# A two-layer sparse graph attention kernel: layer two's variances taken by VectorE's statistics, x added beside the exponential, the last roots on GpSimd, and a new order of work

## The chip, the core and the metric

The kernel runs on one core of a Trainium2 chip. The metric is the device time of one execution in microseconds (us), the median of several runs. The engines are called as in the profile: PE is TensorE, DVE is VectorE, ACT is ScalarE, POOL is GpSimd, and SP starts plain transfers.

## What is computed

Two graph attention layers over one adjacency matrix of 2048 rows, each followed by a residual and a layer norm over 256 channels. Cut to what matters:

```python
def _layernorm(x, axis=-1, eps=1e-05):
    m = jnp.mean(x, axis=axis, keepdims=True)
    v = jnp.var(x, axis=axis, keepdims=True)
    return (x - m) / jnp.sqrt(v + eps)

# layer one: masked dot-product attention with 8 heads over the edges of adj
scores = jnp.where(adj > 0, einsum('hnd,hmd->hnm', q * SCALE, k), NEG_FILL)
out = einsum('hnm,hmd->hnd', softmax(scores), vv)
x = _layernorm(x + out)
# layer two: h = x W^T + b; scores leaky_relu(s_src[i] + s_dst[j]); softmax over the edges
x = _layernorm(x + elu(einsum('ijh,jhd->ihd', attn, h)))
```

## The kernel before

**Tiles.** The 2048 rows are 16 tiles of 128. About one in 200 entries of the matrix is an edge, so the kernel first turns the matrix into lists of edges (MAX8 on DVE, L1693), and then works on chunks of 128 edges: 73 chunks in 7 groups per layer, a group holding the edges of one to four tiles. A stage is named by its kind, layer, group and piece: prod(0,3,0) is the first piece of the products of group 3 in layer one (layers count from 0).

**Layer one, by chunk and tile.** POOL fetches the rows of k and v that a chunk's edges point at by an indirect transfer, a gather (L1214), into a ring of 24 slots. PE copies the query rows to the edges (L1560), DVE multiplies (prod, L1828), POOL halves the products by an addition (half, L1227) and DVE sums them (score, L1839). PE turns the scores, DVE scans for row ends (L1893 to L1898), ACT takes exponentials, DVE weighs the fetched v (weigh, L1931), and PE adds them up per tile (L1612). Weighing frees the ring slot. For each tile DVE divides and adds x (norm, L1656, L1658, L1650), ACT takes the sum of squares (L1403, L1405), POOL takes the root (shift, L1246 to L1253), ACT normalizes (L1418), PE turns the tile (turn_norm, L1623), ACT copies it, PE multiplies it by W (project, L1634, L1636), ACT copies the result out (evac, L1433) and SP stores it in a table in memory. For the last two tiles DVE normalizes (L1944). The queries of a group need a split of x into a high and a low part, which POOL makes (left_1 and left_2, L1235, L1240). A stage `bad` on POOL (L1290 to L1299) gathers the check whether the lists were long enough.

**Layer two.** POOL gathers from the table (L1214 again, ring of 44 slots), so its first gather waits for the last store of layer one. DVE scores, scans and weighs, PE sums. For each tile: norm_a on DVE (L1656, L1658) divides, ACT takes Relu and Exp (elu, L1438, L1441), norm_b on DVE (L1954 makes the elu, L1650 adds x and sums the row), ACT takes the variance (spread_of_b: L1411 the mean, L1413 the squares). For a pair of tiles ACT guesses the inverse root (L1447, L1449), DVE refines it (refine, four small instructions, L1963 to L1969), and ACT writes the normalized tile (emit, L1457), which SP stores.

**What sets the order.** Each engine runs its stages in one fixed order, made by a list scheduler in the program (`Order`, `all_stages`). It ranks a stage by planned durations and by a table `LATER` that shifts the rank of each kind of stage; `AHEAD` and `FORESIGHT` are two more numbers of it. An engine's block takes the stages in that order, and waits on semaphores for what a stage needs; nothing behind a waiting instruction of the same engine can pass it.

## Time and profile before

| | |
|---|---|
| median of three runs | 341.42 us (338.7 to 343.41) |
| the profiled execution: time, span | 341.08 us, 339.5 us |
| outside the span | 1.58 us |
| busy: DVE, PE, POOL, ACT | 264.3, 223.4, 220.6, 172.6 us |
| mean granted clock of PE | 0.852 |

Durations below come from the profiled execution. Layer one runs to about 222 us, where the first gather of layer two starts; that layer's 73 gathers run to 314.5 us, and the last write ends at 339.5 us. In a row of the timeline the first number is the start, the second the duration (of all instructions of the row, where xN is over 1), and the bracket tells how long the engine had been idle and what ended that; "issue" means that the profile shows no releaser.

### The profile page before, as it was taken

How to read it: one execution, taken by the hardware profiler on the slowest of the kernel's cores; microseconds unless marked ns; L12 is line 12 of the kernel's file. 1: busy time of each engine (PE TensorE's matmuls, PEld its weight loads, DVE VectorE, ACT ScalarE, POOL GpSimd, SP SyncE). 2: the span in 40 equal slices, each digit the busy share in tenths (PEclk: the TensorE clock that was granted, in tenths of full speed). 3: DMA queues.
4: the chain of work that ended last, by engine and by line, in shares of the span. 5: the costliest groups of instructions: out<-in, count | busy, mean ns of one | idle time of the engine just before them, and what ended most of it. 6: DMA issues, size and time to landing. Idle time of an engine off the chain costs nothing.

```text
span 339.5 us, 5180 instructions
## 1 busy us (share of the span) xinstructions
PE 223.4 (66%) x1282; PEld 158.0 (47%) x1282; DVE 264.3 (78%) x760; ACT 172.6 (51%) x473; POOL 220.6 (65%) x354
## 2 busy tenths in 40 slices
PE   0099756648685388688888988761714957758850
PEld 0077433436463156466666755450503734536630
DVE  2998999999999489899999766896416388885981
ACT  4646668352867556668643646200020056764495
POOL 8627867726858776787889771167777777777000
PEclk9999695857799679999999999655585899969995
DMA  7977769945886947453535420024434454554212
GB/s 279 384 193 292 258 209 315 336 163 162 270 298 189 323 160 269 124 156 89 165 93 151 105 70 20 33 84 115 108 108 114 108 141 117 133 146 139 64 36 68
DMA packets 23710, 55.90 MB, mean 165 GB/s; under 512 B 6267, under 2 KB 14587, under 8 KB 21627
## 3 DMA queue, kind: packets, MB, share of 16 engines
q0 software_dynamic: 9392, 29.74, 30.5%
q1 hardware_dynamic: 14283, 25.77, 21.8%
q8 instruction: 13, 0.21, 0.3%
q14 instruction: 22, 0.18, 0.2%
HBM read 51.17 MB, written 4.33 MB: 163 GB/s over the span
## 4 chain that ended last, share of the span: by engine, by line
POOL 13%; PE 12%; issue 12%; DVE 10%; ACT 6%; DMA 2%; DVEq 0%; ACTq 0%; POOLq 0%
POOL e_ring L1214 10%; PE e_po L1612 8%; DMA e_ring<-table,e_col_i 2%; DVE e_left L1931 2%; DVE e_weighted L1931 1%; PE e_pj L1636 1%; POOL e_slot_e L1227 1%; DVE e_y L1658 1%; ACT e_search L1320 1%; DVE e_kept L1693 1%; ACT e_prod L1457 1%; DVE e_run L1893 1%; DVE e_run L1895 1%; DVE e_y L1954 1%; PE e_pt L1623 1%
## 5 line engine op out<-in xcount | busy, mean ns | idle before, releaser
L1214 POOL DMA_INDIRECT e_ring<-in_kv,e_col_i x73 | 71.2, 976 | 32.3 <-issue 16.7
L1214 POOL DMA_INDIRECT e_ring<-table,e_col_i x73 | 70.1, 961 | 23.8 <-issue 22.3
L1612 PE MATMUL e_po<-e_weighted,e_sel_edges 128*128 128x264 f32 x178 | 47.3, 402 | 7.0 <-DVE e_weighted L1931 7.0
L1320 ACT ACTIVATE e_search<-e_search 128x2048 bf16<-128x2048 int32 x16 | 39.9, 2491 | 11.4 <-DMA e_search<-in_adj 7.1
L1612 PEld LDWEIGHTS e_po<-e_weighted,e_sel_edges 128*128 128x128 f32 x178 | 32.7, 195 | 14.0 <-DVE e_weighted L1931 9.0
L1560 PE MATMUL e_pq<-e_left,e_sel_rows 128*128 128x256 bf16 x164 | 35.2, 311 | 0.0
L1693 DVE MAX8 e_kept<-e_search 128x8 f32<-128x1024 f32 x24 | 29.4, 1224 | 0.6
L1612 PE MATMUL e_po<-e_left,e_search 128*128 128x264 f32 x92 | 27.3, 452 | 1.7 <-DVE e_left L1931 1.7
L1931 DVE TENSOR_TENSOR e_weighted<-e_ring,e_pc 128x528 f32<-128x528 f32 (+1 forms) x40 | 26.0, 669 | 2.6 <-PE e_pc L1592 1.9
L1599 PE MATMUL e_po<-e_mean_row,e_diagonal 128*128 128x264 f32 x64 | 22.4, 436 | 8.3 <-DVE e_y L1658 7.9
L1356 ACT ACTIVATE e_diagonal<-e_ident,e_filled 128x128 f32<-128x128 f32 x32 | 12.5, 398 | 28.5 <-DVE e_y L1658 28.1
L1560 PE MATMUL e_pq<-e_xres,e_sel_rows 128*128 128x256 bf16 x82 | 25.8, 314 | 0.4 <-DVE e_prod L1853 0.4
L1612 PEld LDWEIGHTS e_po<-e_left,e_search 128*128 128x128 f32 x92 | 20.5, 228 | 6.8 <-DVE e_left L1931 2.6
L1379 ACT COPY e_sel_edges<-e_pt 128x512 f32<-128x512 f32 (+1 forms) x23 | 12.3, 537 | 21.9 <-PE e_po L1612 13.6
L1828 DVE TENSOR_TENSOR e_prod<-e_pq,e_ring 128x512 f32<-128x512 f32 (+1 forms) x27 | 16.3, 634 | 8.1 <-issue 4.9
L1560 PEld LDWEIGHTS e_pq<-e_left,e_sel_rows 128*128 128x128 bf16 x164 | 17.9, 109 | 5.8 <-issue 0.6
L1227 POOL TENSOR_TENSOR e_slot_e<-e_prod 128x256 f32<-128x256 f32 (+1 forms) x27 | 18.5, 702 | 1.6 <-DVE e_prod L1828 1.4
L1395 ACT ACTIVATE e_weight_t<-e_shifted 88x128 f32<-88x128 f32 (+5 forms) x14 | 4.3, 306 | 29.8 <-DVE e_shifted L1898 21.7
L1235 POOL TENSOR_TENSOR e_left<-e_xres 128x256 f32<-128x256 f32 (+3 forms) x7 | 8.1, 1163 | 13.8 <-PE e_pq L1560 7.5
L1599 PEld LDWEIGHTS e_po<-e_mean_row,e_diagonal 128*128 128x128 f32 x64 | 10.5, 196 | 13.3 <-issue 12.4
L1650 DVE SCALAR_TENSOR_TENSOR e_y<-e_y,e_xres 128x256 f32<-128x256 f32 x32 | 14.8, 462 | 1.1
L1585 PE MATMUL e_pc<-e_ident,e_score 128*88 128x128 f32 (+5 forms) x30 | 5.8, 309 | 14.7 <-DVE e_score L1880 10.0
(240 smaller groups left out, 586.3 us busy)
## 6 DMA issues: line engine op xcount, KB each, us to landing
e_search<-in_adj SPq DMA_DIRECT2D x16, 1024.0 KB, 7.1
table<-e_hx SPq DMA_DIRECT2D x16, 136.0 KB, 1.8
e_ring<-in_kv SPq DMA_DIRECT2D x1, 2112.0 KB, 13.3
out<-e_prod SPq DMA_DIRECT2D x16, 128.0 KB, 2.3
e_ring<-in_kv,e_col_i POOLq DMA_INDIRECT x73, 4.1
e_ring<-table,e_col_i POOLq DMA_INDIRECT x73, 2.8
e_xres<-in_x SPq DMA_DIRECT2D x2, 384.0 KB, 9.8
e_xres<-in_x SPq DMA_DIRECT2D x1, 512.0 KB, 8.0
```

Of the source, the lines that this page charges most:

```text
L1214: nc.gpsimd.indirect_dma_start(out=rings[layer][:, q % RING[layer], :], out_offset=None, in_=kv if layer == 0 else table, in_offset=bass.I ...
L1227: nc.gpsimd.tensor_tensor(halves[:, pair % 2, at:at + m * C // 2].rearrange("p (h d) -> p h d", d=D // 2), products[:, :, 0:D // 2], produ ...
L1320: nc.scalar.activation(val_signs[:, k % 2, :], adj_tile[:, k % 2, :], ACT.Sign, accum_out=signs[:, k:k + 1]).then_inc(s("sgn_ready"), 1)
L1356: nc.scalar.activation(diagonal[:, n % 3, :], ident[:], ACT.Copy, scale=filled[:, at:at + 1]).then_inc(s("diagonal_ready"), 1)
L1379: nc.scalar.copy(selection(0, u, m).rearrange("p c r -> p (c r)"), pt[:, 0:m * P]).then_inc(s("turns_copied"), 1)
L1560: last = nc.tensor.matmul(pq[b % 2][:, j * C:(j + 1) * C], sel(u), upper(x_parts[part])[:, 0, :], start=(u == some[0][0] and part == 0), s ...
L1599: nc.tensor.matmul(po[n % 2][:, 0:CV], diagonal[:, n % 3, :], mean_row[:], start=True, stop=False)
L1612: last = nc.tensor.matmul(po[n % 2][:, 0:CV], selection(layer, u, 1)[:, 0, :], weighted[plan.weighed_into(b)][:, j * CV:(j + 1) * CV], sta ...
L1650: return v.scalar_tensor_tensor(out=y[:, k % 4, :], in0=y[:, k % 4, :], scalar=1.0, in1=xres[:, plan.tile_of(layer, k), :], op0=ALU.mult, ...
L1693: last = v.max(to, segs[:, i])
L1828: v.tensor_tensor(prod[:, i % 2, 0:m * C].rearrange("p (c k) -> p c k", c=m), pq[b % 2][:, 0:m * C].rearrange("p (c k) -> p c k", c=m), ri ...
L1931: v.tensor_tensor(weighted[plan.weighed_into(b)][:, 0:m * CV].rearrange("p (c h d) -> p c h d", c=m, d=D1), rings[layer][:, at:at + m, lo: ...
```

## The change

**Layer two.** The stage spread_of_b on ACT is gone. A new DVE stage plus_x adds max(y, 0) to x as soon as norm_a is done, while ACT works on the exponential; norm_b then adds the exponential less one, and takes mean and variance by two statistics instructions, BN_STATS and BN_AGGR (`take_moments`). norm_a of tile k now waits for elu of tile k-4 and no longer for its emit. For the last four tiles a POOL stage `roots` takes the place of guess and refine, and the emit of the last tile is done by DVE.

**Layer one.** The last two tiles take their moments by the same two instructions on DVE, not on ACT. The turn of the last tile is put ahead of the projection of the one before it.

**Order.** `AHEAD`, `FORESIGHT` and the whole table `LATER` have new values (two entries are shown).

```diff
-AHEAD = 11.4
+AHEAD = 11.255
-FORESIGHT = 1.4357
+FORESIGHT = 1.2927
-LATER = {("back", 0): -0.93, ("back", 1): 1.71, ...
+LATER = {("back", 0): -4.69, ("back", 1): 0.94, ...
...
-            put("PE", 1.35 if k < 13 else 2.2, rank - 0.2, ("project", k), ("copy_norm", k), None if bank is None else ("evac", k - 1) ...
+            put("PE", 1.35 if k < 13 else 2.2, rank - 0.2, ("project", k), ("copy_norm", k), ("turn_norm", NK - 1) if k == NK - 2 else None, ...
...
-            put("DVE", 0.7, rank - 0.2, ("norm_a", k), end, ("emit", k - 4) if k >= 4 else ("normed", NK - 4 + k))
+            put("DVE", 0.7, rank - 0.2, ("norm_a", k), end, ("elu", k - 4) if k >= 4 else ("normed", NK - 4 + k))
+            put("DVE", 0.44, rank - 0.2, ("plus_x", k), ("norm_a", k))
...
+def alone(k):
+
+    return k >= len(SLOTS) - 4
...
+                elif stage[0] == "roots":
+                    k = stage[1]
+                    one = slice(k % 4, k % 4 + 1)
+                    pool.wait_ge(s("z_ready"), NT + k + 1)
+                    pool.wait_ge(s("emitted"), k - 3)
+                    own.did(nc.gpsimd.tensor_scalar(var_eps[:, one], moments[:, k % 4, 1:2], EPS, None, ALU.add))
+                    own.wait()
+                    if k == NT - 1:
+                        nc.gpsimd.tensor_tensor(rstd[:, one], var_eps[:, one], minus_half[:], ALU.pow).then_inc(s("rooted"), 1)
+                        continue
...
-                elif stage[0] == "spread_of_b":
-                    k = stage[1]
-                    one = slice(k % 4, k % 4 + 1)
-                    act.wait_ge(s("z_ready"), NT + k + 1)
-                    own.did(nc.scalar.activation(neg_mean[:, one], total[:, one], ACT.Copy, scale=-1.0 / C))
-                    own.wait()
-                    nc.scalar.activation(elu[:, k % 2, :], y[:, k % 4, :], ACT.Square, bias=neg_mean[:, one], accum_out=squares[:, one]).then_inc(s("var_ready"), 1)
...
+            def take_moments(k, z):
+                st.did(v.bn_stats(stats[:, k % 4, :], z))
+                st.wait()
+                v.bn_aggr(moments[:, k % 4, :], stats[:, k % 4, :]).then_inc(s("z_ready"), 1)
...
+                elif stage[0] == "plus_x":
+                    k = stage[1]
+                    z = xres[:, plan.tile_of(1, k), :]
+                    st.did(v.scalar_tensor_tensor(out=z, in0=y[:, k % 4, :], scalar=0.0, in1=z, op0=ALU.max, op1=ALU.add))
                 elif stage[0] == "norm_b":
                     k = stage[1]
                     dve.wait_ge(s("elu_ready"), k + 1)
-                    v.scalar_tensor_tensor(out=y[:, k % 4, :], in0=elu[:, k % 2, :], scalar=-1.0, in1=y[:, k % 4, :], op0=ALU.add, op1=ALU.max).then_inc(s("elu_used"), 1)
+                    if k >= 4:
+                        dve.wait_ge(s("guess_ready"), k // 2 - 1)
+                    st.wait()
+                    z = xres[:, plan.tile_of(1, k), :]
+                    v.scalar_tensor_tensor(out=z, in0=elu[:, k % 2, :], scalar=-1.0, in1=z, op0=ALU.add, op1=ALU.add).then_inc(s("elu_used"), 1)
                     dve.wait_ge(s("elu_used"), k + 1)
-                    with_x(1, k).then_inc(s("z_ready"), 1)
+                    take_moments(k, z)
+                elif stage[0] == "emit" and stage[1] == NT - 1:
...
+                    dve.wait_ge(s("rooted"), 4)
+                    dve.wait_ge(out_stored[k % 2], 16 * (k // 2))
+                    v.tensor_scalar(y_out[:, k % 2, :], xres[:, plan.tile_of(1, k), :], moments[:, k % 4, 0:1], rstd[:, one], ALU.subtract, ALU.mult).then_inc(s("last_emitted"), 1)
```

**First place: POOL in the middle of layer one.** The rows are POOL's instructions in program order; L1227 and L1241 are the halves, L1214 and L1228 the gathers, L1235/L1240 and L1249/L1254 the split of x for a later group, and the three one-column rows are the root of a tile. Before, from the last halves of group 2's second piece to those of its last piece:

```order
L1227 TENSOR_TENSOR e_slot_e<-e_prod 128x256 x2
L1235 TENSOR_TENSOR e_left<-e_xres 128x768
L1240 TENSOR_TENSOR e_left<-e_left 128x768
L1214 DMA e_ring<-in_kv,e_col_i 128x520 x3
L1246 TENSOR_SCALAR e_var_eps<-e_norms 128x1
L1251 TENSOR_TENSOR e_rstd<-e_var_eps,e_minus_half 128x1
L1253 TENSOR_TENSOR e_shift<-e_norms,e_rstd 128x1
L1214 DMA e_ring<-in_kv,e_col_i 128x520
L1227 TENSOR_TENSOR e_slot_e<-e_prod 128x256
L1227 TENSOR_TENSOR e_slot_e<-e_prod 128x128
```

With the change:

```order
L1241 TENSOR_TENSOR e_slot_e<-e_prod 128x256 x2
L1228 DMA e_ring<-in_kv,e_col_i 128x520 x6
L1241 TENSOR_TENSOR e_slot_e<-e_prod 128x256
L1241 TENSOR_TENSOR e_slot_e<-e_prod 128x128
L1264 TENSOR_SCALAR e_var_eps<-e_norms 128x1
L1269 TENSOR_TENSOR e_rstd<-e_var_eps,e_minus_half 128x1
L1271 TENSOR_TENSOR e_shift<-e_norms,e_rstd 128x1
L1228 DMA e_ring<-in_kv,e_col_i 128x520 x4
```

The three gathers and the one behind them (35 to 38, group 3's first four) and two more now stand right behind the halves; the two split instructions have moved behind the next tile's root, and the root behind the halves.

**Second place: POOL at the end of layer one.** The same engine around the last group's halves; L1290 to L1299 (L1321 to L1330) are the stage `bad`. Before:

```order
L1296 TENSOR_TENSOR e_end<-e_end,e_caps 128x16
L1297 TENSOR_SCALAR e_bad<-e_found_n 128x16
L1299 TENSOR_SCALAR e_bad<-e_end 128x16
L1227 TENSOR_TENSOR e_slot_e<-e_prod 128x256 x2
L1227 TENSOR_TENSOR e_slot_e<-e_prod 128x128
```

With the change:

```order
L1241 TENSOR_TENSOR e_slot_e<-e_prod 128x256 x2
L1336 TENSOR_TENSOR e_src_parts<-e_src_parts 128x24
L1338 TENSOR_TENSOR e_src_parts<-e_src_parts 128x24
L1264 TENSOR_SCALAR e_var_eps<-e_norms 128x1
L1269 TENSOR_TENSOR e_rstd<-e_var_eps,e_minus_half 128x1
L1271 TENSOR_TENSOR e_shift<-e_norms,e_rstd 128x1
L1241 TENSOR_TENSOR e_slot_e<-e_prod 128x128
L1321 TENSOR_TENSOR e_end<-e_mid,e_half 128x16
```

The eight instructions of `bad` stood ahead of the last group's halves and now stand behind them.

**Third place: PE between the layers.** The turns of the last two tiles (L1623, L1650, e_xres) and their projections (L1634/L1636, L1661/L1663); L1571 and L1598 spread source terms to the edges. Before:

```order
L1623 MATMUL e_pt<-e_ident,e_xres 128x128 x2
L1634 MATMUL e_pj<-e_w_sb 128x280
L1636 MATMUL e_pj<-e_w_ext,e_xt 128x280 x2
L1623 MATMUL e_pq<-e_ident,e_xres 128x128 x2
L1571 MATMUL e_pt<-e_src_parts,e_sel_rows 128x24 x16
L1634 MATMUL e_pq<-e_w_sb 128x280
L1636 MATMUL e_pq<-e_w_ext,e_count 128x280 x2
```

With the change:

```order
L1650 MATMUL e_pt<-e_ident,e_xres 128x128 x2
L1650 MATMUL e_pq<-e_ident,e_xres 128x128 x2
L1661 MATMUL e_pj<-e_w_sb 128x280
L1663 MATMUL e_pj<-e_w_ext,e_xt 128x280 x2
L1661 MATMUL e_pq<-e_w_sb 128x280
L1663 MATMUL e_pq<-e_w_ext,e_count 128x280 x2
L1598 MATMUL e_pt<-e_src_parts,e_sel_rows 128x24 x16
```

The last turn stands ahead of the projection of tile 14, and the spread of 16 small products no longer stands between the two projections.

## Rows read from the trace of the kernel before

**Rows 1.** Busy time by stretch: stretch, its length, PE, PEld, DVE, ACT, POOL, clock
```profile
0.00:170.00 170.00, 112.98 (x756) 80.20 (x757) 147.83 (x399) 103.40 (x239) 119.68 (x217) 0.88 0.70 232
...
300.00:325.00 25.00, 19.89 (x73) 13.98 (x73) 20.44 (x57) 12.51 (x39) 11.19 (x12) 0.86 0.34 94
```
**Rows 2.** The gathers' line L1214: layer two's shortest/median/longest, and the landing
```profile
L1214 POOL DMA_INDIRECT e_ring<-table,e_col_i x73: 942/946/1250, 222.5 to 313.6; - x73
...
DMA to landing us min/median/max: 2.7/3.5/9.0
```
**Rows 3.** Timeline, POOL: layer two's first and last gather
```profile
222.46 1.20 POOL L1214 DMA_INDIRECT e_ring<-table,e_col_i  x1 [1.90 <-issue]
...
313.60 0.94 POOL L1214 DMA_INDIRECT e_ring<-table,e_col_i  x1 [0.30 <-issue]
```
**Rows 4.** Timeline, DVE, the two halves of prod(0,3,0) in the middle of layer one
```profile
112.43 0.69 DVE L1828 TENSOR_TENSOR e_prod<-e_pq,e_ring 128x512 f32<-128x512 f32 x1
117.99 0.69 DVE L1828 TENSOR_TENSOR e_prod<-e_pq,e_ring 128x512 f32<-128x512 f32 x1 [4.88 <-issue]
```
**Rows 5.** Timeline, POOL ahead of that: halves, left_1, gather 35, gather 38
```profile
95.19 1.45 POOL L1227 TENSOR_TENSOR e_slot_e<-e_prod 128x256 f32<-128x256 f32 x2
100.44 1.47 POOL L1235 TENSOR_TENSOR e_left<-e_xres 128x768 f32<-128x768 f32 x1 [3.80 <-DMA e_xres<-in_x]
...
103.66 0.97 POOL L1214 DMA_INDIRECT e_ring<-in_kv,e_col_i  x1 [0.15 <-issue]
...
108.88 1.07 POOL L1214 DMA_INDIRECT e_ring<-in_kv,e_col_i  x1 [0.56 <-DVE e_weighted L1931]
```
**Rows 6.** The page's DMA issues: layer one's gathers, median us to landing
```profile
e_ring<-in_kv,e_col_i POOLq DMA_INDIRECT x73, 4.1
```
**Rows 7.** Timeline, end of layer one: POOL's last halves, DVE behind them
```profile
198.84 1.89 POOL L1227 TENSOR_TENSOR e_slot_e<-e_prod 128x256 f32<-128x256 f32 x3
...
199.70 0.42 DVE L1828 TENSOR_TENSOR e_prod<-e_pq,e_ring 128x256 f32<-128x256 f32 x1 [1.31 <-POOL e_slot_e L1227]
```
**Rows 8.** Timeline between the layers: normed 15, project 14, turn 15, project 15, evac 15
```profile
213.09 0.41 DVE L1944 TENSOR_SCALAR e_xres<-e_y,e_norms,e_rstd 128x256 f32<-128x256 f32 x1 [0.77 <-POOL e_rstd L1249]
...
213.84 1.33 PE L1636 MATMUL e_pj<-e_w_ext,e_xt 128*128 128x280 f32 x4
214.96 0.63 PE L1623 MATMUL e_pq<-e_ident,e_xres 128*128 128x128 f32 x2
...
216.88 0.41 PE L1634 MATMUL e_pq<-e_w_sb 3*128 3x280 bf16 x1
...
219.53 0.39 ACT L1433 COPY e_hx<-e_pq 128x272 f32<-128x272 f32 x1 [3.27 <-issue]
```
**Rows 9.** Groups by line and shape: busy us, mean ns of one
```profile
L1812 DVE SCALAR_TENSOR_TENSOR e_hit<-e_slot_e,e_rel 128x256 f32<-128x256 f32 x16 | 10.1, 630 | 1.6 <-issue 0.4
...
L1839 DVE TENSOR_REDUCE e_score<-e_slot_e 128x16 f32<-128x256 f32 x1 | 0.4, 414 | 0.0
...
L1721 DVE TENSOR_REDUCE e_full<-e_raw 128x1 f32<-128x8 f32 x2 | 0.3, 167 | 0.1
...
L1710 DVE TENSOR_SCALAR e_hit<-e_val 128x256 f32<-128x256 f32 x1 | 0.3, 295 | 0.0
...
L1246 POOL TENSOR_SCALAR e_var_eps<-e_norms 128x1 f32<-128x1 f32 x16 | 3.2, 201 | 8.8 <-ACT e_count L1405 4.5 <-ACT e_xt L1405 3.3
...
L1249 POOL TENSOR_TENSOR e_rstd<-e_var_eps,e_minus_half 128x1 f32<-128x1 f32 x2 | 1.1, 550 | 0.2
```
**Rows 10.** Timeline, the end: norm_b 15, refine 7, emit 15
```profile
331.45 0.43 DVE L1650 SCALAR_TENSOR_TENSOR e_y<-e_y,e_xres 128x256 f32<-128x256 f32 x1
...
334.26 0.16 DVE L1963 SCALAR_TENSOR_TENSOR e_guessed<-e_norms,e_guess 128x2 f32<-128x2 f32 x1 [2.38 <-ACT e_guess L1449]
...
335.87 0.60 ACT L1457 ACTIVATE e_prod<-e_y,e_shift,e_rstd 128x256 f32<-128x256 f32 x1 [0.23 <-issue]
```
**Rows 11.** Timeline, DVE, one of layer one's small waits for POOL
```profile
142.55 1.02 DVE L1828 TENSOR_TENSOR e_prod<-e_pq,e_ring 128x512 f32<-128x512 f32 x2 [0.86 <-POOL e_slot_e L1227]
```

More of the change, by code:

```diff
@@ new lines @@
+LATER = {("back", 0): -4.69, ("back", 1): 0.94, ("copy_mean", 0): 0.08, ("copy_mean", 1): 7.98, ("diagonal", 0): 19.08,
+         ("diagonal", 1): 0.03, ("exp", 0): 5.74, ("exp", 1): -0.11, ("fill", 0): 4.26, ("fill", 1): -0.92, ("gather", 0): 2.18,
+         ("gather", 1): 2.1, ("scan", 0): 0.02, ("scan", 1): 14.06, ("score", 0): -1.57, ("score", 1): -0.45, ("sums", 0): 2.35,
+         ("sums", 1): 14.26, ("turn", 0): -3.72, ("turn", 1): -2.01, ("weigh", 0): 6.78, ("weigh", 1): -0.27, "add_src": 1.65,
+         "bad": 0.02, "bad_sum": -5.35, "check": 13.99, "choose": -2.09, "column_sums": 4.03, "copy_big": -5.38, "copy_edges": 3.29,
+         "copy_norm": 3.11, "copy_pens": 5.43, "count": -5.36, "elu": -18.39, "emit": -25.38, "evac": 20.21, "far": -1.36,
+         "filled": -2.01, "find": -8.36, "find_big": -10.39, "flags": 4.95, "guess": -0.76, "half": -2.59, "left_1": -0.25,
+         "left_2": -0.99, "load": -7.31, "mean_h": 5.3, "mean_v": 72.47, "move": 9.22, "move_big": 4.8, "norm": -1.34, "norm_a": 4.61,
+         "norm_b": 0.53, "normed": 21.18, "out": -0.71, "pack": -9.28, "place": 0.32, "plus_x": 24.4, "prefix": 0.49, "prod": -1.67,
+         "project": 3.43, "queries": -4.05, "refine": -13.89, "roots": -2.3, "rows": 26.71, "select": 5.78, "shift": -22.35,
+         "sign": -0.71, "split_b": -1.6, "spread": 7.38, "spread_of": 2.59, "store": 1.87, "sum_w": -1.64, "turn_edges": -11.83,
+         "turn_norm": -12.27, "turn_pens": 1.88, "turn_src": 12.43, "v": -28.34, "w": 45.38, "x": 12.17}
@@ L980, in edge_pass @@
         xts = [sb("e_xt", [P, C]), count0]
+        stats = sb("e_stats", [P, 4, 6])
+        moments = sb("e_moments", [P, 4, 2])
         norms = sb("e_norms", [P, 3, 4])
@@ L1968, in _ @@
                     st.wait()
-                    v.tensor_tensor(shift[:, two], neg_mean[:, two], rstd[:, two], ALU.mult).then_inc(s("refined"), 1)
+                    v.scalar_tensor_tensor(out=shift[:, two], in0=moments[:, two, 0], scalar=-1.0, in1=rstd[:, two], op0=ALU.mult, op1=ALU.mult).then_inc(s("refined"), 1)
                     dve.wait_ge(s("refined"), j + 1)
```

91 lines of the change are left out of this document (51 added, 40 removed).

## Prediction

> **What bounds the kernel now.** I read the busy times by stretch first, to see which engine is full where; then the line of the gathers, for layer two; then DVE's and POOL's timelines at DVE's longest waits.
>
> In layer one DVE is the bound: 147.8 of the first 170 us, against 119.7 on POOL and 113.0 on PE [rows 1]. There a wait of DVE costs its length, and a shuffle of other engines' work costs nothing unless it makes DVE wait.
>
> Layer two is bound by its gathers until they end. All 73 take 0.94 to 1.25 us [rows 2], the first starts at 222.46 and the last at 313.60 [rows 3]: 91.1 us over 72 steps is 1.27 each, one behind the other, and the wait ahead of one is "issue", not a ring slot. So layer two starts when the last store of layer one has landed, its gathers take 92 us whatever DVE does, and an engine's work is free there if it is done by the last chunk. Then comes a tail of 25 us in which DVE is full again, 20.4 of 25 us from 300 [rows 1].
>
> So three places set the end: DVE's waits in layer one, the bridge from the last tile to the first gather, and the tail. I sum against the profiled execution's own 341.08 us (span 339.5 and 1.58 outside it); it lies 0.3 under the median of 341.42, so the sum is the forecast of the median within that.
>
> **The change, part by part.**
>
> *A. The middle of layer one.* DVE's longest wait there is 4.88 us ahead of the second half of prod(0,3,0) [rows 4], which multiplies chunk 38. Gather 38 is issued at 108.88 [rows 5]; the longest landing of a gather is 9.0 us [rows 2], and 108.88 + 9.0 = 117.9 is where the product starts. It was late because POOL, done with its halves at 95.19 + 1.45 = 96.64, stood 3.80 us waiting for x's next part before left_1, and then did left_1 and left_2 before gather 35 at 103.66 [rows 5]. With the change gathers 35 to 40 stand right behind the halves, the split behind shift 1. From 96.64 at 1.25 each, 38 could go at 100.4; I take 103, since the ring's slots come free only as DVE weighs. By the reordered queue DVE reaches the product at about 109.7. At the median landing of 4.1 [rows 6] the rows are there at 107.1 and the wait is gone: −4.9. At 9.0 again they land at 112.0 and 2.3 us remain: −2.6. I take −4.9: six gathers that no longer come in a crowd behind a stopped queue are nearer to the median than to the longest landing. The split that moved back is covered: group 4's products start at 142.55 [rows 11], 26 us after its new place (about 116.5: six gathers, halves, a root, four gathers, two halves, flags, a root and 3.0 us of split behind 96.64).
>
> *B. The end of layer one.* DVE waits 1.31 us for the last group's halves [rows 7], which stand on POOL behind `bad`. The halves now go first; `bad` has no reader before the end of the layer's bridge. −1.3; bounds 0 (the halves wait for the products anyway) and −1.3.
>
> *C. The bridge.* Turn 15 starts at 214.96 behind projection 14, projection 15 at 216.88 behind the spread products, evac 15 at 219.53, the first gather 2.93 us after that [rows 8, 3]. But normed 15, which turn 15 needs, ends at 213.09 + 0.41 = 213.50, and projection 14 at 215.17 [rows 8]. With the turn ahead of projection 14, turn 15 runs at 213.5, its copies are done while projection 14 runs, and projection 15 follows at 215.2 rather than 216.88: −1.7. Moments on DVE put 0.41 + 0.16 on each of the two tiles (prices below), but save ACT's squares, so normed 15 stays where it was within 0.1. I take −1.4, as the copies share ACT with evac 14; bounds 0 (copy late) and −1.7.
>
> *D. Layer two's tiles and the tail.* Neither BN_STATS nor BN_AGGR is in the trace. BN_STATS reads 256 elements a partition: below, a one-source operation on 256, 0.295; above, the accumulating one on 256, 0.63; I take the reduction of 256, 0.41, as the nearest in kind [rows 9]. BN_AGGR reads six numbers: 0.17 as a reduction of eight [rows 9]. plus_x and the sum in norm_b are the 0.43 to 0.46 of norm_b's instruction [rows 10]. Per tile DVE did 0.43 + 0.46 = 0.89 and now does 0.45 + 0.46 + 0.41 + 0.04 + 0.16 = 1.52: +0.63. Ten tiles' worth lies ahead of the score of the last but one group in the new order, beside the gathers; DVE has room there, and I put +0.5 for what it delays. Six come after it: +3.8. Refine runs twice before the last norm_b instead of three times, −0.8 (four of 0.16 with gaps). Two waits for turned scores, covered before, lie open: +0.6 as an estimate of 0.3 each. So norm_b 15 ends 4.1 later than 331.88 [rows 10], at 336.0 in old time.
>
> From there to the end of emit 15 it was 336.47 − 331.88 = 4.6 us: ACT's means and squares of two tiles, guess, refine (DVE waited 2.38) and two emits [rows 10]. Now it is POOL's 0.20 and 0.55 [rows 9] with 0.17 for two handovers, then DVE's emit of 0.41 as L1944 [rows 8] and 0.1: 1.4. So −3.2, and D is +4.1 − 3.2 = **+0.9**. With BN_STATS at 0.295 six tiles give −0.7, D is +0.2; at 0.63 they give +1.3, D is +2.2.
>
> *E. New waits.* The whole order of layer one is new. Waits of DVE of the size of 0.86 and 1.31 [rows 11, 7] are what such an order leaves; I allow **+1.3**, one or two of them, between 0 and +2.6.
>
> *Spread_of_b on ACT*, 0.9 a tile, is removed at no gain besides the tail: ACT is not full in layer two (12.5 of 25 us [rows 1]).
>
> **Sum:** 341.08 − 4.9 − 1.3 − 1.4 + 0.9 + 1.3 = **335.7 us**.
>
> **A lock that would speak against it.** DVE's comparisons (one source each) run beside the first gathers of layer two, its weighing (two sources) beside the last; yet the slowest of the 73 took 1.25 us against a median of 0.946, and the last 0.94 [rows 2, 3]. So no operation of DVE has held a gather up by more than 0.30, nearly all by nothing, and I put the moments' effect on POOL at 0. The Trainium skill (SBUF — State Buffer, "🔬 SBUF: two separate sides") says that a DVE operation in a two-port mode locks GpSimd out of a shared port, so that a gather's descriptors cannot be written. By that rule ten BN_STATS beside the gathers would each hold one up; the trace agrees only to the 0.30 above. Which mode BN_STATS uses no row here shows, so the hold-up is a rival.
>
> **The rivals.**
>
> 1. *No new waits, and some old ones go too.* The small waits behind A are a lottery that the new table draws again. For it: DVE's idle time from 120 to 200 comes in pieces like rows 11. Without E and with two of them gone (2.3): 335.7 − 1.3 − 2.3 = **332.1**.
>
> 2. *The stall moves.* Gather 38 lands in time, but DVE, 4.9 us ahead, meets the next late transfer or half: the gathers behind it keep POOL's pace. For it: POOL is at 70% in the same stretch [rows 1] and ring slots are freed by DVE's own weighing. A is worth nothing: 335.7 + 4.9 = **340.6**; with half of it, 338.2.
>
> 3. *Slower: the moments hold up the gathers.* If each of the ten BN_STATS beside gathers costs POOL one more issue of 0.95 [rows 2], the last gather is 9.5 us later, and 335.7 + 9.5 = **345.2**. It decides from 0.54 us a tile on (5.4 gained, ten tiles). Against it: no operation beside the gathers has cost one more than 0.30.
>
> 4. *The tail only.* BN_STATS far above 0.63 would be paid six times at the end; 5.4 us are used up at 0.9 more, at 1.3 us each. Against it: no row on 256 elements is above 0.63.
>
> **Chances.** My forecast, between 333.5 and 338: 0.50. Rival 1, 330 to 333.5: 0.19. Rival 2, 338 to 342: 0.25. Rivals 3 and 4, above 342: 0.06. To leave out no more than 2 in 10 the range goes from 331.5 to 341.0: it takes in A at −2.6 (338.0), BN_STATS at either bound (335.0, 337.0) and rival 2. It holds faster and unchanged alike, so the likeliest case's own range stands beside it: 333.5 to 338. 2% of 341.4 is 6.8 us, about what a measurement of this kernel can tell from no change; faster by that is below 334.6: rival 1 and a third of the forecast's case, 0.19 + 0.17 = 0.36. Slower is above 348.2: 0.02. The rest, 0.62, is within 2%.
>
> **What the changed profile would show.** A: gather 38 at about 103, no DVE wait over 1 us ahead of prod(0,3,0); if one stands there, the landing was the cause, and if it stands a group later, rival 2. B: the last halves ahead of `bad`, and no wait for them on DVE. C: turn 15 before projection 14, evac 15 about 1.4 us nearer to normed 15. D: BN_STATS near 0.41 and BN_AGGR near 0.17; norm_b 15 to the last emit 1.4 us; gathers still 1.25 apart and the stretch from the first gather to the last 91 us (rival 3 if more); from the last gather to the end of the last emit 336.47 − 313.60 + 0.9 = 23.8 us. I would be wrong if layer one ends less than 4 us earlier, or if DVE falls behind the gathers so far that they wait for ring slots.

## The result

| | before | changed |
|---|---|---|
| median of four runs | 340.62 us (338.70 to 343.41) | 345.46 us (343.39 to 347.10) |
| ratio, with its 95% interval | | 1.0139 (1.0090 to 1.0187) |
| the profiled execution: time, span | 341.08, 339.5 us | 344.15, 342.4 us |
| busy: DVE, PE, POOL, ACT | 264.3, 223.4, 220.6, 172.6 us | 276.9, 226.1, 226.4, 159.0 us |

I had forecast 335.7 us, and the changed kernel is 1.4% slower. Both halves of the picture changed: layer two does start earlier, by 4.0 us of the 6.3 I had summed, and everything behind its last gather takes 6.8 us longer, where I had written 0.9. These are the rows of the changed kernel that answer to [rows 3] and [rows 10]. First its timeline: POOL's first and last gather, and what DVE does from the score of the last but one group to the last write.

```profile
218.47 1.12 POOL L1228 DMA_INDIRECT e_ring<-table,e_col_i  x1 [1.64 <-issue]
...
309.84 0.94 POOL L1228 DMA_INDIRECT e_ring<-table,e_col_i  x1 [0.30 <-issue]
...
310.45 0.25 DVE L1908 TENSOR_TENSOR e_score<-e_src,e_ring 128x88 f32<-128x88 f32 x1 [0.41 <-issue]
...
334.21 0.18 DVE L1679 BATCH_NORM_AGGREGATE e_moments<-e_stats 128x2 f32<-128x6 f32 x1
...
335.50 0.41 DVE L2008 TENSOR_SCALAR e_prod<-e_xres,e_moments,e_rstd 128x256 f32<-128x256 f32 x1 [1.11 <-POOL e_rstd L1280]
```

In the kernel before, the same score and the end of the last moments (ACT's squares followed) stand here:

```profile
311.24 0.25 DVE L1876 TENSOR_TENSOR e_score<-e_src,e_ring 128x88 f32<-128x88 f32 x1 [0.17 <-issue]
...
331.80 0.08 DVE L1650 DVE_READ_ACCUMULATOR e_y<-e_y,e_xres 128x1 f32 x1
```

Then the instructions that close the changed program, from the view of the line that holds them all (count, shortest/median/longest in ns, start; "q" is an engine's sequencer):

```profile
L2048 POOLq DRAIN  x1: 6362/6362/6362, 335.8 to 335.8; - x1
L2048 ACTq DRAIN  x1: 81/81/81, 337.0 to 337.0; - x1
L2048 DVEq DRAIN  x1: 58/58/58, 338.6 to 338.6; - x1
L2048 SPq DRAIN  x1: 53/53/53, 338.8 to 338.8; - x1
```

The last write ends at 335.91, earlier than the 336.47 of before. SP has stored it and is done at 338.8. But the span ends at 342.44, 0.23 us behind POOL's closing instruction, a DRAIN that takes 6.36 us from 335.85, to 342.21. In the kernel before, whose lines follow, POOL was through with its last gather at 314.55 and closed at 320.92, 6.37 later, in the shade of the tail; there the span ended 0.21 us behind SP's DRAIN.

```profile
L1997 POOLq DRAIN  x1: 8793/8793/8793, 312.1 to 312.1; - x1
...
L1997 SPq DRAIN  x1: 53/53/53, 339.2 to 339.2; - x1
```

With the roots, POOL's last work is among the last of all.

The difference of the two spans, stretch by stretch (us, from the two timelines):

| stretch | before | changed | difference | my sum |
|---|---|---|---|---|
| to the first gather of layer two | 222.46 | 218.47 | −3.99 | −6.3 |
| first gather to last gather | 91.14 | 91.37 | +0.23 | 0 |
| last gather to the score of the last but one group | −2.36 | +0.61 | +2.97 | +0.5 |
| that score to the last moments | 20.64 | 23.94 | +3.30 | +3.6 |
| last moments to the end of the last write | 4.59 | 1.52 | −3.07 | −3.2 |
| last write to the end of the span | 2.98 | 6.53 | +3.55 | 0 |
| **sum** | 339.45 | 342.44 | **+2.99** | −5.4 |

Two rows carry the miss of the tail: the score comes 2.97 later against the gathers, and the end 3.55 later against the last write. The first row is the miss of layer one. And the medians lie 4.84 apart where the profiled executions lie 3.07: of the four changed runs two took 343.4 and 344.2, two 346.8 and 347.1, and the profiled one is of the shorter pair. Ratios here and below leave out executions that took over 1.5% longer than the fastest of the same kernel. The experiments take these one by one.

### The profile page after: what moved, and what is told of

The parts are those of the page before. It is cut to its first block, busy times and chain, and to the rows that moved or that the text cites. A ratio compares the mean times of both kernels' runs of the same rounds, so it can differ in the third digit from the quotient of the medians.

```text
span 342.4 us, 5152 instructions
## 1 busy us (share of the span) xinstructions
PE 226.1 (66%) x1282; PEld 159.9 (47%) x1282; DVE 276.9 (81%) x773; ACT 159.0 (46%) x414; POOL 226.4 (66%) x365
## 4 chain that ended last, share of the span: by engine, by line
DVE 28%; PE 19%; POOL 10%; issue 9%; ACT 1%; DMA 1%; DVEq 1%; POOLq 0%; ACTq 0%
PE e_po L1639 11%; POOL e_ring L1228 7%; DVE e_kept L1725 3%; PE e_pj L1663 3%; DVE e_y L1690 2%; DVE e_weighted L1963 2%; DVE e_prod L1860 2%; DVE e_stats L1677 2%; DVE e_xres L1999 2%; DVE e_run L1925 2%; DVE e_run L1927 1%; DVE e_left L1963 1%; DVE e_rden L1688 1%; DVE e_xres L1991 1%; PE e_po L1626 1%
## 5 line engine op out<-in xcount | busy, mean ns | idle before, releaser
L1228 POOL DMA_INDIRECT e_ring<-in_kv,e_col_i x73 | 71.8, 983 | 32.3 <-issue 18.6
L1228 POOL DMA_INDIRECT e_ring<-table,e_col_i x73 | 70.4, 964 | 23.6 <-issue 21.7
L1639 PE MATMUL e_po<-e_weighted,e_sel_edges 128*128 128x264 f32 x178 | 50.0, 418 | 9.1 <-DVE e_weighted L1963 9.1
L1639 PEld LDWEIGHTS e_po<-e_weighted,e_sel_edges 128*128 128x128 f32 x178 | 34.1, 204 | 16.4 <-DVE e_weighted L1963 11.1
L1639 PE MATMUL e_po<-e_left,e_search 128*128 128x264 f32 x92 | 31.4, 503 | 1.8 <-DVE e_left L1963 1.8
L1639 PEld LDWEIGHTS e_po<-e_left,e_search 128*128 128x128 f32 x92 | 23.2, 258 | 8.2 <-DVE e_left L1963 2.8
L1461 ACT ACTIVATE e_left<-e_y 128x256 f32<-128x256 f32 x16 | 6.6, 411 | 33.1 <-DVE e_y L1690 33.1
L1241 POOL TENSOR_TENSOR e_slot_e<-e_prod 128x256 f32<-128x256 f32 (+1 forms) x27 | 18.5, 705 | 0.7 <-DVE e_prod L1860 0.4
L1510 PE MATMUL e_pl<-e_slot_hi,e_sel_rows 128*128 128x20 bf16 (+2 forms) x82 | 5.2, 175 | 18.0 <-DVE e_slot_lo L1800 9.4
L1249 POOL TENSOR_TENSOR e_left<-e_xres 128x256 f32<-128x256 f32 (+3 forms) x7 | 8.2, 1167 | 12.6 <-PE e_pq L1587 10.3
L1688 DVE RECIPROCAL e_rden<-e_po 128x8 f32<-128x8 f32 x32 | 6.5, 204 | 11.3 <-PE e_po L1639 10.7
```

Of the source, the lines that this page charges most:

```text
L1228: nc.gpsimd.indirect_dma_start(out=rings[layer][:, q % RING[layer], :], out_offset=None, in_=kv if layer == 0 else table, in_offset=bass.I ...
L1241: nc.gpsimd.tensor_tensor(halves[:, pair % 2, at:at + m * C // 2].rearrange("p (h d) -> p h d", d=D // 2), products[:, :, 0:D // 2], produ ...
L1639: last = nc.tensor.matmul(po[n % 2][:, 0:CV], selection(layer, u, 1)[:, 0, :], weighted[plan.weighed_into(b)][:, j * CV:(j + 1) * CV], sta ...
L1688: st.did(v.reciprocal(rden[:], sums[:, :, D]))
```

## The experiments

**1. POOL's closing instruction, taken away and added.** The changed kernel without its roots on POOL, and the kernel before with one POOL instruction late:

```diff
 def alone(k):
-    return k >= len(SLOTS) - 4
+    return False
...
-                    dve.wait_ge(s("rooted"), 4)
+                    dve.wait_ge(s("refined"), NT // 2)
```

> The changed kernel without the roots on POOL: guess and refine to the last tile, everything else as changed (DVE still writes the last tile). Theory: the end is held by POOL, whose closing instruction took 6.36 us behind its last root (335.85 to 342.21, span 342.4). With no root, POOL closes behind the last gather, at about 310.7 + 6.4 = 317, and the end goes by the last write: the last moments at 334.4, ACT's guess 0.8, refine 0.75, the write 0.4 and handovers, so 336.5, and 3.0 behind it as before: a span of 339.6, a time near 341.3, against 344.15 for the changed kernel's own profile. Rival: the stretch behind the last write is long because DVE writes it and loads its flag just ahead of it; then the span is 342.4 + 0.7 = 343.1 and POOL has nothing to do with it.

```diff
+            pool.wait_ge(s("refined"), NT // 2)
+            nc.gpsimd.memset(var_eps[:, 0:1], 0.0)
```

> The kernel before with one more POOL instruction behind its last gather: a memset of one column that waits for the last refine (335.0 in the profile of before); nothing reads it. Theory (POOL's closing instruction costs 6.4 us behind POOL's last work, whatever that was): POOL's last work ends at 335.3, it closes at 341.7, span 341.9 instead of 339.5, time 343.5. Rival (the end goes by the last store alone): span 339.5 and time 341.1, as the memset lies beside the last write.

The closing instructions of POOL in these two, the first without the roots, the second of before with the late memset, and the memset itself:

```profile
L2048 POOLq DRAIN  x1: 7768/7768/7768, 309.6 to 309.6; - x1
```

```profile
L2000 POOLq DRAIN  x1: 6362/6362/6362, 337.9 to 337.9; - x1
```

```profile
336.88 0.10 POOL L1310 MEMSET e_var_eps<- 128x1 f32 x1 [20.68 <-DVE e_shift L1972]
```

Without the roots POOL closes at 317.38, 6.37 behind its last gather, and the end goes by the store again: 3.18 us from the last write to the end of a span of 341.20. The median is 343.05, ratio 1.0057 (1.0011 to 1.0102), against 1.0139. My figure of 339.6 for the span was 1.6 too low: guess and refine put 2.9 us between the last moments and the last write, not 2.1, and a pair's refine stands ahead of them, +0.8. So the roots on POOL shorten the chain by 2.1 us (338.02 − 335.91; 1.9 when counted from the last gather) and lengthen the end by 3.35.

The memset of 0.10 us makes POOL close at 337.86 + 6.36 = 344.22 in a span of 344.45; the last write of that run ended at 338.28, so the end lies 6.17 behind it, where it was 2.98. It moved the end by 3.2 us, though nothing reads what it writes. The one execution took 346.08 us where I had expected 343.5: layer two started 1.36 us later than in the profile of before, and the DRAIN began 0.88 us behind the memset. Both rivals are out: the end does not go by the last store alone, and DVE's write and flag are not what lengthens it. What made POOL late was once its roots and once a memset; other work of POOL was not tried.

**2. Is the late score made by the ten tiles' statistics?** BN_STATS on 8 channels in the first ten tiles (their variances are then those of 8 channels):

```diff
-            def take_moments(k, z):
-                st.did(v.bn_stats(stats[:, k % 4, :], z))
+            def take_moments(k, z, few=False):
+                st.did(v.bn_stats(stats[:, k % 4, :], z[:, 0:8] if few else z))
...
-                    take_moments(k, z)
+                    take_moments(k, z, few=k < 10)
```

> The changed kernel, but in the first ten tiles of layer two BN_STATS reads 8 of the 256 channels, so that their variances are those of 8 channels; the last six tiles are whole. Theory: the ten tiles ahead of the score of the last but one group are not hidden beside the gathers; they make DVE late, so that this score starts 0.65 us behind the start of the last gather, where it stood 2.36 ahead of it in the kernel before. Ten times (0.43 - 0.17) = 2.6 us less work then puts the score 2 to 2.6 us nearer and the end with it: span about 340.0. Rival: the score is late for PE's sums and the new order of weighing, not for the statistics; then it stays where it was against the last gather, within 0.3, and the span stays at 342.4.

```profile
308.94 0.25 DVE L1908 TENSOR_TENSOR e_score<-e_src,e_ring 128x88 f32<-128x88 f32 x1 [0.42 <-issue]
...
310.99 0.95 POOL L1228 DMA_INDIRECT e_ring<-table,e_col_i  x1 [0.30 <-ACT e_prod L1484]
```

Timeline of that run: the score now stands 2.05 ahead of the last gather, where it stood 0.61 behind it. That is 2.66 us for 2.6 us of work taken away (BN_STATS took 0.17 us instead of 0.43 in ten tiles), and the end moved with it: 29.94 us behind the start of the last gather instead of 32.60. As far as these two profiles go, the statistics of the first ten tiles cost the end their full length. The span was 340.93 and not the 340.0 I had written, with a first gather 1.2 us later.

**3. Code or order?** The change has two halves that can be crossed: the code, and the three sets of numbers that set the order. Each alone:

```diff
 # the kernel before, with
-AHEAD = 11.4
+AHEAD = 11.255
-FORESIGHT = 1.4357
+FORESIGHT = 1.2927
-LATER = {("back", 0): -0.93, ...
+LATER = {("back", 0): -4.69, ...
```

> The kernel before with the three sets of numbers of the changed one (AHEAD, FORESIGHT, LATER) and no other edit, so that only the order of work is new. Theory: the 4.0 us by which layer two started earlier (first gather 218.5 instead of 222.5) are the order's for the most part (the wait of 4.88 is gone by it), and the tail of before is kept: first gather at 219 to 220.5, span 336.5 to 338, ratio 0.99. Rival: the gain is the code's at the end of layer one (moments on DVE, turn of the last tile first); then the first gather stays at 221.5 to 222.5 and the ratio at 1.00.

> The changed kernel with the three sets of numbers of the kernel before, so that its code is new and its order goes by the old table. Theory: the late tail comes with the code (plus_x and the statistics on DVE, the root on POOL), not with the order: the score of the last but one group starts 0 to 1 us behind the start of the last gather, the end is 31.5 to 33 us behind the last gather's start, POOL closes 6.36 us behind its last root; and the bridge is short with the code alone, so the first gather is at 218.5 to 220.5. Span 341.5 to 344. Rival: the new order made the tail; then the score stands 2 us ahead of the last gather and the end is 29 to 30 us behind it, span near 339.5.

The four profiles side by side (us; the last three columns count from the start of the last gather, or from what their head says):

| code | numbers | first gather | score | last gather to end | last write to end | ratio |
|---|---|---|---|---|---|---|
| old | old | 222.46 | −2.36 | 25.85 | 2.98 | 1 |
| old | new | 223.67 | −1.84 | 27.76 | 3.00 | 1.0112 (1.0076 to 1.0149) |
| new | old | 221.23 | −2.10 | 30.39 | 6.53 | 1.0144 (1.0081 to 1.0208) |
| new | new | 218.47 | +0.61 | 32.60 | 6.53 | 1.0139 (1.0090 to 1.0187) |

Either half alone is as slow as both. The tail has 4.5 to 4.8 us of the code and 1.9 to 2.2 of the numbers, and they add up within 0.3 us; 3.55 of the code's part is POOL's close. With the old numbers the ten tiles' statistics are hidden as I had said (the score moves by 0.26, and the last write stands 23.86 behind the last gather, +0.99 to before's 22.87; I had +0.9). With both, the score comes 2.97 later, where the code alone moved it by 0.26 and the numbers alone by 0.52: the new numbers use up that room, and then the statistics lie open. Both of my expectations fell. The new numbers were to bring layer two's start forward and to keep the tail of before; alone they bring the start 1.2 us later and the end of the tail 1.9 us later. And the late score was to come with the code; with the old numbers it came 2.10 ahead of the last gather, as the rival had it, and the first gather at 221.23, later than the 218.5 to 220.5 that I had.

**4. Layer two's numbers alone.** The changed kernel with the numbers of layer two's stages as before:

> The changed kernel with the numbers of layer two's stages in LATER as before (plus_x and roots as changed). Theory: the score of the last but one group moves from 0.6 us behind the start of the last gather to about 2 ahead of it, as in the run with the whole old table, and the end from 32.6 to 30.4 us behind that start; POOL still closes 6.36 us behind its last root, so the span is 340 to 341 (first gather 218.5 to 219.5). Rival: the lateness of DVE is of the code, and the score stays within 1 us of the last gather: span 342 to 343.

The score starts at 308.46, 1.98 ahead of the last gather at 310.44, so the same code is not late with layer two's old numbers. The end lies 31.45 behind the last gather's start, not the 30.4 I had; POOL's DRAIN took 6.36 us as in the changed kernel, and the time of the one execution was 343.51. So layer two's numbers are worth 1.15 of the 2.2 us at the end (32.60 − 31.45). The other 1.06, to the 30.39 with all old numbers, goes with those that this run left new, AHEAD, FORESIGHT and layer one's; how is open.

**5. What made layer two start earlier?** The bridge alone, in the kernel before:

```diff
-            ..., ("copy_norm", k), None if bank is None else ("evac", k - 1) ...
+            ..., ("copy_norm", k), ("turn_norm", NK - 1) if k == NK - 2 else None, None if bank is None else ("evac", k - 1) ...
```

> The kernel before with one constraint for the scheduler: the turn of the last tile stands ahead of the projection of tile 14 (the order of a few neighbouring stages in the last 30 us of layer one shifts with it; all else is as before). Theory: of the changed kernel's 4.0 us at the first gather nearly all is this bridge: from the start of normed 15 to evac 15 it took 6.44 us before and 3.67 in the changed kernel, where PE's granted clock stayed at 1.00 instead of 0.65 and projection 15 took 1.21 us instead of 2.23. The tail of before is kept (25.9 us from the start of the last gather to the end). First gather 219 to 220, span 336 to 337.3, ratio 0.991. Rival: the 4.0 us are from DVE's moments in the last two tiles and from the wait removed in the middle; then the first gather stays at 221.5 to 222.5 and the ratio at 1.00.

Ratio 1.0010 (0.9977 to 1.0043), first gather 222.20: nothing gained, though PE does what the change has it do. Compare the two bridges, first that run's and then that of the changed kernel: normed 15, the two projections, evac 15.

```profile
212.51 0.41 DVE L1945 TENSOR_SCALAR e_xres<-e_y,e_norms,e_rstd 128x256 f32<-128x256 f32 x1 [0.57 <-POOL e_rstd L1250]
...
214.82 2.23 PE L1637 MATMUL e_pj<-e_w_ext,e_xt 128*128 128x280 f32 x4
...
217.33 1.90 PE L1637 MATMUL e_pq<-e_w_ext,e_count 128*128 128x280 f32 x4
...
219.26 0.39 ACT L1434 COPY e_hx<-e_pq 128x272 f32<-128x272 f32 x1 [1.68 <-PE e_pq L1637]
```

```profile
211.88 0.41 DVE L1981 TENSOR_SCALAR e_xres<-e_y,e_moments,e_rstd 128x256 f32<-128x256 f32 x1 [0.58 <-POOL e_rstd L1267]
...
212.94 1.21 PE L1663 MATMUL e_pj<-e_w_ext,e_xt 128*128 128x280 f32 x4
...
214.30 1.21 PE L1663 MATMUL e_pq<-e_w_ext,e_count 128*128 128x280 f32 x4
...
215.55 0.39 ACT L1456 COPY e_hx<-e_pq 128x272 f32<-128x272 f32 x1 [0.86 <-PE e_pq L1663]
```

A projection takes 1.21 us in one and 2.23 and 1.90 in the other. The busy times by stretch, of the changed kernel, of the bridge alone, and of the new code with the old numbers, end in three numbers: PE's granted clock, the share of time in which the DMA engines were busy, and GB/s:

```profile
212.00:216.00 4.00, 3.55 (x28) 2.29 (x28) 4.00 (x22) 1.99 (x12) 0.33 (x1) 1.00 0.15 51
```

```profile
212.00:216.00 4.00, 3.15 (x22) 1.98 (x23) 2.68 (x13) 1.25 (x8) 0.92 (x3) 0.50 0.11 35
```

```profile
212.00:216.00 4.00, 3.51 (x10) 1.59 (x8) 3.55 (x18) 1.42 (x9) 0.58 (x3) 0.60 0.00 0
```

In the changed kernel PE keeps its full clock (2.4 GHz) until 221.2, behind the bridge; in the bridge alone it has half of it (1.2 GHz) from 211.9, in the kernel before from 214.8. Over all profiles of this study the time from normed 15 to evac 15 falls into two groups: 3.66 or 3.67 us in the seven where the clock fell at 219.8 or later, and 6.1 to 7.5 us in those where it fell between 211.9 and 214.8, whichever kernel it was. The two kernels of experiment 7 below make the cleanest pair, as both have the changed kernel's layer one, instruction for instruction: 3.67 us in the profile of the first, with the full clock until 221.5, and 6.21 in that of the second, with half of it from 213.96. These are turn 14 (the last turn but one of the bridge), the two projections and evac 15 of the second:

```profile
213.18 0.44 PE L1649 MATMUL e_pt<-e_ident,e_xres 128*128 128x128 f32 x2 [0.89 <-DVE e_xres L1980]
...
215.13 2.23 PE L1662 MATMUL e_pj<-e_w_ext,e_xt 128*128 128x280 f32 x4
...
217.63 2.23 PE L1662 MATMUL e_pq<-e_w_ext,e_count 128*128 128x280 f32 x4
...
219.91 0.39 ACT L1459 COPY e_hx<-e_pq 128x272 f32<-128x272 f32 x1 [2.01 <-PE e_pq L1662]
```

So the clock alone was worth 2.54 us of that bridge. Why it falls ahead of the bridge or behind it is open. PE stood still ahead of turn 14 for 1.56 us in the bridge alone and for 1.41 in the kernel before, and for 0.89 in the changed kernel. But it stood still for the same 0.89 in both profiles of the pair, and in the old code with the new numbers (experiment 3) the clock fell at 213.62 with no wait there. All that can be said is a count: of the eight profiles with the changed kernel's layer one, two of them with idle transposes added, seven kept the full clock through the bridge, and of the six with another layer one none did.

**6. Parts of the change that cost DVE nothing.** The bridge and the last write by DVE beside ACT's write of tile 14, no statistics:

```diff
-            put("ACT", 0.52, rank - 0.3, ("emit", k), ...
+            put("DVE" if k == NK - 1 else "ACT", 0.42 if k == NK - 1 else 0.52, rank - 0.3, ("emit", k), ...
```

> The kernel before with two parts of the change that cost DVE next to nothing: the last turn ahead of projection 14, and the write of the last tile by DVE beside ACT's write of tile 14 (ACT loads its flag ahead of that). No statistics, no plus_x, nothing on POOL in the tail. Theory: the bridge gives 2.5 to 3 as in the run beside it, and the end 0.8 more (the last write ended at 336.47, 1.43 behind refine; with both engines it is over 0.6 behind it): span 335.3 to 336.5, ratio 0.985 to 0.990. Rival: the last store, not the last write, sets the end, since two stores issued together share the queue: then it ends as the run beside it, within 0.3.

Ratio 0.9989 (0.9962 to 1.0017). The tail is 26.5 us from the last gather, not shorter. The last write ended at 338.01 and its store was issued at 339.83, 1.82 later, where SP was 0.80 behind ACT's write before: between the two stores SP loads its flag. The gain of 1 to 1.5% that I had expected did not come, and the rival holds for the end: SP sets it.

**7. New layer one, old tail.** With layer one instruction for instruction as changed, layer two's tiles as before; first with the old numbers for layer two's stages, then with the new ones:

```diff
 # the changed kernel, in layer two
-            put("DVE", 0.44, rank - 0.2, ("plus_x", k), ("norm_a", k))
-            put("DVE", 1.0, rank - 0.2, ("norm_b", k), ("elu", k), ("plus_x", k), ...
+            put("DVE", 0.84, rank - 0.2, ("norm_b", k), ("elu", k))
+            put("ACT", 0.87, rank - 0.3, ("spread_of_b", k), ("norm_b", k))
...
```

> The changed kernel's layer one, instruction for instruction, with layer two's tiles as in the kernel before (variances by ACT, guess and refine to the end, no plus_x, no root on POOL, ACT writes the last tile), and the numbers of layer two's stages in LATER as before. Theory: the changed kernel's early start of layer two (first gather at 218.5 to 219.7 in three profiles) and the tail of before (25.9 to 26 us from the start of the last gather to the end) add up: span 335.5 to 337, ratio 0.985 to 0.992. Rival: the early start needs DVE's statistics only in layer one and is kept, but the tail of before was short only because its gathers came later (DVE is the bound of the whole of layer two, so that an earlier first gather does not bring the end forward); then the score of the last but one group starts behind the last gather, and the span is 338.5 to 339.5, ratio 1.00.

> As the run beside it, but the numbers of layer two's stages in LATER as changed too, so that only the code of layer two's tiles is as before. Theory: the new numbers cost the tail about 2 us with the old code too (27.8 us from the start of the last gather to the end where only the numbers were new, 25.9 where neither was): span 337 to 339, 1.5 to 2 more than the run beside it. Rival: the tail's 2 us there came from something else in that kernel (a late bridge), and both runs have the same tail within 0.5.

Profile of the first: first gather 218.64, score 2.35 ahead of the last gather, end 27.07 behind it, span 337.56, the shortest of the study (I had expected 335.5 to 337). Its times, though, fall into two groups, eight of 338.5 to 340.2 and four of 342.5 to 343.9, and the ratio is 0.9972 (0.9936 to 1.0008): no difference that can be told from none. The second gave 0.9991 (0.9951 to 1.0031); the two intervals overlap, so that what the numbers cost the tail is not settled by this pair. The profile of the second is that of its longest execution, 344.21 us, and is the one with the bridge of 6.21 us above.

**8. Keeping PE busy.** Seven transposes that nothing reads, where PE would wait for normed 14 and 15, in that kernel and in the changed one:

```diff
                     k = stage[1]
+                    if k >= NT - 2:
+                        pe.wait_ge(s("queries_read"), plan.batch0[1, 0])
+                        for j in range(5 if k == NT - 2 else 2):
+                            nc.tensor.transpose(norm_bank(NT - 1)[:, 0:P], ident[:], ident[:])
                     pe.wait_ge(s("normed"), k + 1)
```

> The run with the new layer one and the old tail, with seven transposes of the identity more on PE that nothing reads (five ahead of the wait for normed 14, two ahead of the wait for normed 15), 0.2 us each at full clock, so that PE does not stand idle there. Theory: that kernel's times fall into two groups (338.5 to 340.2 and 342.5 to 343.9) because PE's granted clock falls to half either ahead of the bridge or behind it; with PE kept busy it stays full through the bridge: the upper group goes, all times within 338 to 341, ratio 0.990 to 0.995, first gather 218.5 to 219.7. Rival: the groups have another cause (transfers that land late in layer one); then a third of the times stays above 342.

> The changed kernel with the same seven transposes. Its four times were 343.4 and 344.2, and 346.8 and 347.1. Theory: the upper two are executions in which PE's clock fell ahead of the bridge; with PE kept busy nearly all times are 343 to 344.7, ratio near 1.007, so that of the slowdown of 1.39% about half is the clock's and the rest the tail's. Rival: a third or more of the times stays above 346.

In the first no time of the upper group came: twelve times of 339.7 to 341.9, three of them above the 341 that I had set. It is paid for at the lower end, where the shortest time is 339.69 instead of 338.53, and the ratio stays 0.9972 (0.9940 to 1.0004), not the 0.990 to 0.995 I had. In the changed kernel the rival's condition came true: four of six times are 343.9 to 344.9 and two, a third, are 346.5 and 346.7, ratio 1.0101 (1.0048 to 1.0153). That the clock in the bridge makes the spread of these kernels fits the profiles and the first run; it is not shown, since four long times in twelve against none in twelve may be chance, and the second run leaves a part of the spread open.

## Why the prediction was wrong, step by step

**What bounds the kernel** was read rightly for two of three stretches: layer two's gathers run one behind the other at 1.27 us (91.37 us from first to last, 91.14 before), and an earlier first gather brings the last one forward by as much. Rival 3, the hold-up of gathers by the statistics, did not come: the slowest of the 73 took 1.24 us and the median 0.947. Of the rule that I cited there (the Trainium skill, "SBUF — State Buffer", "🔬 SBUF: two separate sides") no effect of BN_STATS on a gather is seen here.

**A, the wait of 4.88 us,** went as I had said: gather 38 is issued at 103.39, and the two halves of the product run at once. This is the row that answers to [rows 4]:

```profile
110.05 1.29 DVE L1860 TENSOR_TENSOR e_prod<-e_pq,e_ring 128x512 f32<-128x512 f32 x2
```

But normed 15, at the end of layer one, came only 1.21 earlier (213.09 to 211.88), for A, B and E together, which I had summed to 4.9. **The step that failed** is the sentence that in layer one a shuffle of other engines' work costs nothing unless it makes DVE wait. These are DVE's busy times up to normed 15, of the kernel before and of the changed one (stretch, its length, DVE, then clock and DMA as above):

```profile
0.00:213.09 213.09, 180.54 (x481) 0.90 0.62 202
```

```profile
0.00:211.88 211.88, 184.85 (x484) 0.90 0.62 203
```

DVE's idle time fell from 32.55 to 27.03, by 5.5 us, which is more than my 4.9. Its busy time grew by 4.3, which I had put at nothing. The statistics of the last two tiles are 1.2 of it. The other 3.1 are the same instructions, as many as before, taking longer. Between 60 and 211 us the kernel before has six instructions of DVE that took over 0.2 us longer than the shortest of their kind in any profile, and they lost 2.8 us; the changed kernel has 13, and they lost 6.0. All six, and 12 of the 13, ran beside arithmetic on POOL (the last section shows one). No run took that arithmetic away, so that it is the cause of the whole 3.1 is read from the rows and not shown.

The idle time includes a new wait of 2.45 us near the end of layer one, for weights that PE had not turned because ACT took the exponential late, behind a normed that waited for POOL's root:

```profile
186.33 0.60 ACT L1441 ACTIVATE e_xres<-e_y,e_shift,e_rstd 128x256 f32<-128x256 f32 x1 [1.74 <-POOL e_shift L1271]
...
188.80 0.31 ACT L1426 ACTIVATE e_weight_t<-e_shifted 88x128 f32<-88x128 f32 x1
...
190.03 1.32 DVE L1963 TENSOR_TENSOR e_weighted<-e_ring,e_pc 128x528 f32<-128x528 f32 x2 [2.45 <-PE e_pc L1619]
```

Rival 2, the stall that moves, came true in that one wait, but it is not what took the gain. Four profiles of the old code, in which DVE, ACT and POOL have the same order up to 200 us (before, experiments 1, 6 and 5), say the same of the old wait: it was 4.88, 1.80, 2.55 and under 0.5 us, and normed 15 started at 213.09, 213.44, 214.27 and 212.51. The end of layer one does not follow that wait.

**B** showed no wait for the last halves any more, but its 1.31 is inside the same 1.21.

**C, the bridge,** had the right sign, half of the size that was measured (−1.4 for −2.77), and the wrong reason. My sum moved projection 15 forward and left it as long as it was, 2.23 us at half clock. With the clock fallen, the new order took 6.75 us in the bridge alone and 6.21 in the second kernel of experiment 7, against 6.44 before. So 2.54 of the 2.77 are the clock of the profiled execution (6.21 to 3.67). My sum did not have the clock, and that the term came out larger than forecast was luck.

**D, the tail,** failed in two steps: "+0.5 for ten tiles beside the gathers", and the close of POOL, which I had put at nothing. Its prices were near. BN_STATS took 0.428 and BN_AGGR 0.182 (I had 0.41 and 0.16), plus_x 0.417:

```profile
L1677 DVE BATCH_NORM_STATS2 e_stats<-e_xres 128x6 f32<-128x256 f32 x16 | 6.8, 428 | 0.6
...
L1991 DVE SCALAR_TENSOR_TENSOR e_xres<-e_y,e_xres 128x256 f32<-128x256 f32 x16 | 6.7, 417 | 0.3
L1679 DVE BATCH_NORM_AGGREGATE e_moments<-e_stats 128x2 f32<-128x6 f32 x18 | 3.3, 182 | 0.6
```

The six open tiles cost +3.30 (I had +3.6) and the shorter chain gave −3.07 (−3.2). "+0.5 for ten tiles beside the gathers" holds with the old numbers (+0.26) and became +2.97 with the new ones: I priced the new code in the old order's room. And the work moved to POOL was costed as a chain of 0.9 us alone, where its close added 3.55 to the end. I read POOL's idle tail as free, and did not look at what each engine does between its last instruction and the end of the span; the 6.37 us of its closing stood in the trace of before, hidden behind the tail, in a line that is not counted as busy.

**E, +1.3 for new waits,** was large enough: 6.2 us of waits were to go, 5.5 of idle time went, so that new waits took 0.7 net, though one of 2.45 came in one piece.

With the terms as measured (1.21 for A, B and E together) the sum is 341.08 − 1.21 − 2.77 + 0.23 + 2.97 + 3.30 − 3.07 + 3.55 = 344.08, and 344.15 was the profiled time (the rest lies outside the spans). The median, 345.46, is 1.3 us above that execution; its other executions were not profiled.

## What to carry to other kernels

Before work is moved to an idle engine late in a program, look at how that engine closes: here POOL's close ended 6.7 us behind the end of its last root and 7.2 behind that of a late memset, so that POOL's last work must be over that long before the end. A wait of the busiest engine is worth its length only if the engine's busy time stays as it was: compare busy and idle time up to the same instruction, and look through other profiles of the same code in which the wait happens to be shorter. And code and order are to be priced together: room beside a bound is there only in the order in which it was read.

## What was not expected of the hardware

POOL's DRAIN took 6.362 us in each of the six profiles with late POOL work, and began 0.38 us behind the last root or 0.88 behind the memset. It ended 6.37 us behind the last gather in the eight without. The closing DRAINs of ACT, DVE and SP took 0.05 to 0.09.

PE's granted clock decides the bridge by 2.5 us with the same instructions (3.67 us at full clock, 6.21 at half of it). It fell ahead of the bridge in seven of 14 profiles and behind it in the other seven, and with the same layer one and the same waits of PE ahead of the last two turns it did either.

Small instructions of DVE can be held while POOL adds. In the changed kernel a CAST of 60 numbers a partition, which takes 0.19 to 0.34 us in other places and profiles, took 1.04 and ended 0.06 behind an addition on POOL that had started first:

```profile
120.23 1.52 POOL L1254 TENSOR_TENSOR e_left<-e_left 128x768 f32<-128x768 f32 x1
...
120.77 1.04 DVE L1798 CAST e_slot_hi<-e_slots 128x60 bf16<-128x60 f32 x1
```

The eight profiles in which that addition started 0.54 us ahead of this CAST all have it at 1.03 to 1.04 us; in the changed kernel with the old tail and the idle transposes (experiment 8), with no arithmetic of POOL beside it, it took 0.19. The Trainium skill ("SBUF — State Buffer", "🔬 SBUF: two separate sides") says that the port pair shared by DVE and GpSimd is held for a whole instruction by whichever starts first, of a GpSimd operation and a DVE operation in a two-port mode or with two inputs in SBUF, and that the other blocks; these two rows agree, but in which mode the CAST ran no row here shows.
